# Chosen tokens: probabilities divided before their transposes, the attention result made transposed by four heads side by side, the down product in one piece

## The chip, the cores and the metric

The kernel runs on one core of one Trainium2 chip. A core has five engines with a queue each, which meet only through semaphores: TensorE (PE; its weight loads are shown apart as PEld), VectorE (DVE), ScalarE (ACT), GpSimd (POOL) and SyncE (SP), which here only starts DMAs. The metric is the device time of one execution in microseconds, the median of several runs.

## The reference, cut to what matters

The program has two halves. The first is a state-space scan over 16 batches of 1024 tokens by 512 features; the change does not touch it. The second takes, in each of the 16 batches, the 127 tokens with the highest router weight, and runs one transformer layer over them (b = 16, kc = 127, H = 16 heads of hd = 32, D = 512, F = 2048):

```python
x_sel = x[bidx, sel_idx]                      # 127 rows of each batch
hn = rmsnorm(x_sel, ln1)                      # x is layer-normed ahead of this
q = rope(heads(hn @ wq), pos_sel)
kk = rope(heads(hn @ wk), pos_sel)
v = heads(hn @ wv)
sc = jnp.einsum('bhqd,bhkd->bhqk', q, kk) / np.sqrt(hd) + m_sel[:, None]
a = jax.nn.softmax(sc, axis=-1)
o = jnp.einsum('bhqk,bhkd->bhqd', a, v).transpose(0, 2, 1, 3).reshape(b, kc, d) @ wo
x1 = x_sel + o
x2 = x1 + jax.nn.gelu(rmsnorm(x1, ln2) @ w1) @ w2
proc = x2 * w_sel[..., None]                  # scattered back to its rows
```

All is float32, and matrix products are float32 too.

## The kernel before, in words

`scan_phase` is the first half. `ffn_phase` is the second, and the change lies in it alone. It keeps all weights in SBUF and works on one batch a step. One `body(i, par)` for each engine is written out by hand, in the order in which that engine is to issue; a loop of `steps` runs it for i = 0 to 16. Step i does the attention of batch i and, interleaved with it, the MLP of batch i - 1: `attention(i)` is false in step 16 alone, `mlp(i)` in step 0 alone, and `final(i)` is true in step 15, which has no next batch to get ready. The middle steps run from a hardware loop, two at a time. `par` is the parity, and chooses between two buffers; `pm` is the other one.

There is no scheduler. Every PSUM bank has a list of its uses in a step (`BANK_USES`), and a pair of semaphores: `full[bank]` counts how often PE has filled it, `free[bank]` how often a reader has given it back. `fill` makes PE wait until the use before has been read, `filled` makes a reader wait until the use is there. `use_number` turns a step and a use into the count.

In a step PE does this, in this order (`turn` is four 128x128 transposes, `product` four accumulated matmuls):

- q and k of batch i, from `hnT`, which the step before left;
- `h2T` and the four up products `up0` to `up3` (MLP of batch i - 1); ACT makes the gelu of each;
- transposes of the gathered mask rows and of q and k, the mask product and the scores of all 16 heads (`scores`, four heads beside each other, each on 32 rows of the array);
- 16 transposes of the gelu's result (`gT0` to `gT3`), then three quarters of the down product: `down(i, 0)` to `down(i, 2)`;
- 16 transposes of the exponentials `prob` (`aT`), which wait for ACT's exp (`exp_ready`), and the four of the next batch's normed rows (`turn_hn`);
- the last quarter `down(i, 3)`, and meanwhile ACT and DVE copy one half each of the transposed exponentials to `probT`;
- `o`: 16 matmuls, head by head, with `probT` (127 x 128) held in the array and 32 columns of the values `vsb` moved through. The result has tokens on partitions and is not yet divided by the softmax sum;
- half of the next batch's `values`, the four transposes of `osb`, the other half of `values`, and the output product `attn` = `oT` times `w_o`.

DVE in the meantime adds the mask to the scores, takes the row maximum and subtracts it; ACT takes exp; DVE runs `prepare(i + 1)` (layer norm and RMS norm of the next batch's rows, in turn with ACT's `prepare`), copies its half of `probT`, sums `prob` over keys (`mx[:, 1]`), takes the reciprocal, and then divides while it copies `o` from PSUM to `osb`. ACT copies the transposed `osb` to `oT` (`copy(i, "oT", oT[:])`), after the next batch's values (`copy_v`). The semaphore `soft` counts four steps of the softmax in each batch (`SOFT = 4`); `o_ready` counts two: the `probT` copy of DVE and the division.

After `attn`, DVE adds the residual, DVE and ACT make the second norm (`h2`), and the step is at its end; q and k of the next step cover that on PE.

Of the kernel before, what the change touches and what calls it, by code (L numbers as in the profile page):

```python
# [7 lines left out]
ALU = mybir.AluOpType  # L8
# [7 lines left out]
P = 128  # L16
# [65 lines left out]
def scan_phase(nc, semaphores, x, A_log, w_xproj, w_dt, dt_b, D_col, router_w, router_b, ident_c, nsum_c, bc_dram,  # L82
# [824 lines left out]
KS = K - 1  # L907
# [13 lines left out]
    "t1": ["h2T", "up1", "up3", "GT1", "gT1", "gT3", "oT"],  # L921
# [23 lines left out]
def ffn_phase(nc, semaphores, w_dram, x1_dram, out, mask, pos, wq, wk, wv, wo, w1, w2, ln1, ln2, ident_c, sel16_c, token_c,  # L945
              batch_c, inv_c):

    with ExitStack() as ctx:
# [51 lines left out]
        osb = sb("osb", [P, D])  # L1000
# [174 lines left out]
        def _(pe):  # L1175
# [54 lines left out]
            def body(i, par):  # L1230
# [40 lines left out]
                if mlp(i):  # L1271
                    for j in range(4):

                        bank = BANK_OF[f"up{j}"]
                        pe.wait_ge(free[bank], use_number(i, f"up{j}") + 1)
                        fill(pe, i, f"gT{j}")
                        turn(BANK_OF[f"gT{j}"], act_up[:, j * HALF:(j + 1) * HALF])
                    fill(pe, i, "down")
                    for j in range(3):
                        down(i, j)  # L1280
                if attention(i):

                    pe.wait_ge(exp_ready, a + 1)
                    fill(pe, i, "aT")
                    for h in range(H):
                        last = pe.transpose(banks["s"][0:KS, h // 4, (h % 4) * P:(h % 4 + 1) * P], prob[:, h, 0:KS],  # L1286
                                            ident[:])
                    last.then_inc(full["s"], 1)
                    if not final(i):
                        turn_hn(i)  # L1290
                if mlp(i):

                    down(i, 3)
                if attention(i):

                    pe.wait_ge(free["s"], use_number(i, "aT") + 1)
                    pe.wait_ge(o_ready, a * 2 + 1)

                    pe.wait_ge(free["t0"], use_number(i - 1, "v") + 1)
                    fill(pe, i, "o")  # L1300
                    for h in range(H):
                        hd = 4 * (h % 4) + h // 4
                        last = pe.matmul(one["m0"][:, hd * HD:(hd + 1) * HD], probT[0:KS, h, :],  # L1303
                                         vsb[0:KS, par, hd * HD:(hd + 1) * HD], start=True, stop=True)
                    last.then_inc(full["m0"], 1)

                    if not final(i):
                        values(i, range(0, 2))
                    pe.wait_ge(o_ready, a * 2 + 2)
                    fill(pe, i, "oT")  # L1310
                    turn("t1", osb)
                    if not final(i):
                        values(i, range(2, KD))
                    pe.wait_ge(free["t1"], use_number(i, "oT") + 1)
                    fill(pe, i, "attn")
                    product("m1", oT, lambda k: w_o[:, k, :], KD)
# [5 lines left out]
        def _(act):  # L1322
# [52 lines left out]
            def body(i, par):  # L1375
# [14 lines left out]
                if attention(i):  # L1390
# [11 lines left out]
                    if not final(i):  # L1402
                        copy_ahead(i, pm)
                        copy_v(i, pm)
                    copy(i, "oT", oT[:])
# [10 lines left out]
        def _(dve):  # L1416
# [41 lines left out]
            def prepare(a, par):  # L1458

                v = v1[:, par, :]  # L1460
                at = a * NORM
                c = lambda j: v[:, j:j + 1]
# [16 lines left out]
                V.scalar_tensor_tensor(c(0), c(6), 0.25, c(5), ALU.mult, ALU.add).then_inc(norm, 1)  # L1479
                dve.wait_ge(norm_act, a * 5 + 2)  # L1480
                newton(norm, at + 8, c(2), c(0), c(3), c(4), c(6))
                V.tensor_scalar(xn[:, par, :], xg[:, par, :], c(1), c(6), ALU.subtract, ALU.mult).then_inc(norm, 1)

                dve.wait_ge(norm_act, a * 5 + 3)
                V.tensor_scalar(c(9), c(8), 1.0 / D, 1e-6, ALU.mult, ALU.add).then_inc(norm, 1)
# [15 lines left out]
            prepare(0, 0)  # L1501
# [60 lines left out]
            def body(i, par):  # L1562
                a, m, pm = i, i - 1, 1 - par
                if attention(i):
# [30 lines left out]
                    if not final(i):  # L1595
                        prepare(i + 1, pm)
                if attention(i):
                    at = a * SOFT
                    dve.wait_ge(full["s"], use_number(i, "aT") + 1)
                    V.tensor_copy(probT[0:KS, 8:16, :],  # L1600
                                  banks["s"][0:KS, 2:4, :].rearrange("p j (k t) -> p (j k) t", t=P))\
                     .then_inc(o_ready, 1)
                    dve.wait_ge(exp_ready, a + 1)
                    V.tensor_reduce(mx[:, 1, :], prob[:, :, 0:KS], AX.X, ALU.add).then_inc(soft, 1)
                    dve.wait_ge(soft, at + 3)
                    V.reciprocal(mx[:, 2, :], mx[:, 1, :]).then_inc(soft, 1)
                    bank = filled(dve, i, "o")
                    dve.wait_ge(soft, at + 4)

                    V.tensor_tensor(osb[:].rearrange("p (k j e) -> p k j e", k=4, j=4),  # L1610
                                    one[bank].rearrange("p (k j e) -> p k j e", k=4, j=4),
                                    mx[:, 2, :].rearrange("p (j k) -> p k j", j=4).unsqueeze(3)
                                    .to_broadcast([P, 4, 4, HD]), ALU.mult).then_inc(o_ready, 1)
                    dve.wait_ge(o_ready, a * 2 + 2)
                    dve.sem_inc(free[bank], 1)
# [31 lines left out]
SOFT = 4  # L1647
# [77 lines left out]
```

## Time and profile before

| | us |
|---|---|
| median of 3 runs | 4733.67 (4727.59 to 4733.85) |
| the profiled execution's own time | 4730.44 |
| its span on the core | 4728.3 |
| PE busy in the span | 2806.7 (59%) |
| DVE busy | 3868.9 (82%) |
| ACT busy | 2752.0 (58%) |
| POOL busy | 3543.6 (75%) |

The shares are means over both halves. The page's second part cuts the span into 40 slices of 118 us and gives each engine's busy share in tenths: up to about 3640 us DVE and POOL stand at 9 and PE at 4 to 6, and in the last eight slices PE stands at 9 and POOL at 0. The granted clock of PE, in tenths of full speed, is in the same part: 5 to 6 in the first half, 9 in the second. The second half of the program begins near 3640 us, its steps near 3736 us. The rows further down are from the second half, except where their heading says otherwise.

### The profile page before, as it was taken

What the parts mean: (1) busy time and instruction counts of PE and PEld (TensorE: products, weight loads), DVE (VectorE), ACT (ScalarE), POOL (GpSimd) and SP (SyncE); (2) the same over time, 40 slices, a digit from 0 to 9 for tenths busy, and PEclk for the clock granted to TensorE, in tenths of its full rate; (3) what the DMA queues carried; (4) which work ended last, traced back from release to release, by engine and by line L of the source; (5) the groups of instructions that cost most, each with busy time, mean ns of one, the idle gap of its engine ahead of it and who ended that gap; (6) DMA issues with size and microseconds to landing.
All of it is one profiled execution on the core that took longest, in us unless ns stands there. A gap on an engine that the chain in (4) does not pass through costs nothing. (4 is left out here: it accounts for less than half of the span.)

```text
span 4728.3 us, 57323 instructions
## 1 busy us (share of the span) xinstructions
PE 2806.7 (59%) x15590; PEld 1068.8 (23%) x15590; DVE 3868.9 (82%) x3306; ACT 2752.0 (58%) x4103; POOL 3543.6 (75%) x1796
## 2 busy tenths in 40 slices
PE   3555464546464645555454546464642399999997
PEld 1111111111121111111111111111110255555553
DVE  3999999999999999999999999999997644444442
ACT  5676766766767667676766766767754222222221
POOL 4999999999999999999999999999995100000000
PEclk7556565656565656556565656565655599999998
DMA  4454545364544545454545364545533200000000
GB/s 101 96 130 116 142 104 154 85 160 100 147 114 129 131 112 133 111 130 116 141 105 155 82 160 100 146 112 133 135 93 114 82 14 18 18 18 18 18 18 7
DMA packets 198209, 472.73 MB, mean 100 GB/s; under 512 B 60688, under 2 KB 61200, under 8 KB 197088
## 3 DMA queue, kind: packets, MB, share of 16 engines
q1 hardware_dynamic: 177136, 452.11, 37.8%
q0 software_dynamic: 20736, 16.88, 1.3%
q8 instruction: 120, 1.97, 0.2%
q14 instruction: 217, 1.78, 0.1%
HBM read 126.83 MB, written 73.43 MB: 42 GB/s over the span
## 5 line engine op out<-in xcount | busy, mean ns | idle before, releaser
L879 POOL TENSOR_TENSOR ch<-hid,cmat 128x1024 f32<-128x1024 f32 x1024 | 2387.2, 2354 | 101.0 <-DVE hid L733 84.1
L733 DVE TENSOR_TENSOR_SCAN hid<-decay,inp 128x1024 f32<-128x1024 f32 x1024 | 2289.2, 2274 | 96.3 <-ACT decay L600 94.2
L600 ACT ACTIVATE decay<-delr,a_neg 128x1024 f32<-128x1024 f32 x1024 | 1136.7, 1112 | 811.8 <-DVE hid L733 801.0
L399 PE MATMUL ps_y<-ch,nsum 128*32 128x256 f32 x8192 | 1000.3, 588 | 854.9 <-POOL ch L879 850.9
L722 DVE TENSOR_TENSOR inp<-dx,bmat 128x1024 f32<-128x1024 f32 x832 | 959.3, 1211 | 63.2 <-ACT dx L608 63.2
L399 PEld LDWEIGHTS ps_y<-ch,nsum 128*32 128x32 f32 x8192 | 249.0, 143 | 1591.5 <-POOL ch L879 1364.2
L408 PE MATMUL ps_y<-ident,ysb 128*128 128x128 f32 x512 | 168.9, 431 | 683.3 <-ACT ysb L615 666.7
L844 POOL TENSOR_TENSOR inp<-dxr,bmat 128x1024 f32<-128x1024 f32 x192 | 452.4, 2356 | 0.0
L1133 POOL DMA_INDIRECT out_rows<-row,idx_out x16 | 41.1, 2570 | 458.9 <-issue 252.4
L394 PE MATMUL ps_y<-xhT,dskip 128*32 128x256 f32 x2048 | 271.9, 623 | 142.5 <-DVE xr L743 142.5
L408 PEld LDWEIGHTS ps_y<-ident,ysb 128*128 128x128 f32 x512 | 71.3, 196 | 909.4 <-ACT ysb L615 865.9
L608 ACT ACTIVATE dx<-dxr 128x1024 f32<-128x1024 f32 x256 | 260.8, 1019 | 3.0 <-DMA dxr<-dxT 3.0
L382 PE MATMUL aux<-xpT,dtw 64*128 64x512 f32 x256 | 238.9, 1030 | 21.2 <-ACT dxT L510 20.5
L1195 PE MATMUL ps_t<-w,h2T 128*128 128x512 f32 x512 | 226.1, 600 | 11.9 <-ACT h2T L1334 11.9
L1219 PE MATMUL ps_m<-w,gT 128*128 128x512 f32 x512 | 224.9, 592 | 0.0
L1099 POOL COPY idx_x<-cols_i 128x1 uint32 (+1 forms) x16 | 4.7, 297 | 252.8 <-DMA out_rows<-row,idx_out 175.4
L547 ACT ACTIVATE squares<-xr,m 128x512 bf16<-128x512 f32 x256 | 181.7, 713 | 1.0
L853 POOL TENSOR_TENSOR tu<-tu,te 128x1024 f32<-128x1024 f32 x64 | 150.8, 2356 | 36.4 <-ACT tu L524 36.4
L1573 DVE TENSOR_SCALAR GT<-ps_t 128x512 f32<-128x512 f32 x32 | 22.0, 691 | 185.7 <-PE ps_t L1190 185.7
L743 DVE TENSOR_TENSOR xr<-xr,ps_y 128x256 f32<-128x256 f32 x256 | 106.3, 415 | 76.0 <-PE ps_y L408 68.3
L541 ACT ACTIVATE squares<-xr 128x512 bf16<-128x512 f32 x256 | 157.4, 617 | 14.3 <-DVE xr L743 14.2
L1099 POOL COPY idx_m<-cols_i 128x1 uint32 (+1 forms) x16 | 2.9, 180 | 207.3 <-PE ps_t L1190 204.7
(167 smaller groups left out, 3921.7 us busy)
## 6 DMA issues: line engine op xcount, KB each, us to landing
dxr<-dxT SPq DMA_DIRECT2D x1024, 128.0 KB, 2.4
delr<-delT SPq DMA_DIRECT2D x1024, 128.0 KB, 2.4
xr<-in_x SPq DMA_DIRECT2D x32, 1024.0 KB, 5.5
bmat<-b_and_c SPq DMA_DIRECT2D x256, 128.0 KB, 3.4
cmat<-b_and_c SPq DMA_DIRECT2D x256, 128.0 KB, 2.9
x_rows<-xr SPq DMA_DIRECT2D x16, 2048.0 KB, 7.6
out_rows<-xr SPq DMA_DIRECT2D x32, 1024.0 KB, 4.3
w<-in_w SPq DMA_DIRECT2D x2, 4096.0 KB, 23.7
```

The source lines that it names most:

```text
L382: pe.matmul(aux[:], dtw[:, k * P:(k + 1) * P], xpT[0:R, h * HALF:(h + 1) * HALF], start=True, stop=True).then_inc(aux_full, 1)
L394: pe.matmul(ps_y[q * CH:(q + 1) * CH, 0:2 * P], dskip[:, k, c % NT * CH:(c % NT + 1) * CH], xhT[:, i, j, q * 2 * P:(q + 1) * 2 * P], start ...
L399: last = pe.matmul(ps_y[q * CH:(q + 1) * CH, 0:2 * P], nsum[:], ch[:, g, q * 2 * P:(q + 1) * 2 * P], start=False, stop=(g == GROUPS - 1))
L408: last = pe.transpose(ps_y[:, (2 + t) * P:(3 + t) * P], ysb[:, t * P:(t + 1) * P], ident[:])
L600: nc.scalar.activation(decay[:, g % 2, :], delr[:, c % 2, :], ACT.Exp, scale=a_neg[:, i:i + 1])\
L608: nc.scalar.activation(dx[:], dxr[:, c % 2, :], ACT.Copy).then_inc(dx_ready, 1)
L722: nc.vector.tensor_tensor(inp[:, g, :], dx[:], bmat[:, g, :], ALU.mult).then_inc(inp_ready, 1)
L733: nc.vector.tensor_tensor_scan(hid[:, g, :], decay[:, g % 2, :], inp[:, g, :], 0.0, ALU.mult, ALU.add).then_inc(hid_ready, 1)
L844: nc.gpsimd.tensor_tensor(inp[:, OWN, :], dxr[:, c % 2, :], bmat[:, OWN, :], ALU.mult)\
L879: nc.gpsimd.tensor_tensor(ch[:, g, :], hid[:, g, :], cmat[:, g, :], ALU.mult).then_inc(ch_ready, 1)
L1195: last = pe.matmul(one[bank], xT[:, k, :], w(k), start=(k == 0), stop=(k == n - 1))
L1219: last = pe.matmul(one["m1"], gT[:, k, :], w_2[:, k, :], start=(k == 0), stop=(k == F // P - 1))
```

## The change

It has four parts.

1. The exponentials are divided by their sum before PE transposes them. DVE's sum and reciprocal move ahead, and a multiply of the whole `prob` by the reciprocals (128 x 2032 elements) is new; PE's transposes `aT` wait for it (`soft` at 5, where they waited for `exp_ready`). `prepare` on DVE is cut into four functions, whose instructions are laid around the sum and the multiply; ACT's part of it is as it was.
2. `o` changes its operands' roles: 32 columns of `vsb` are held in the array and the 128 columns of `probT` are moved. The result of head 4k + j lands on partitions 32j to 32j + 31, columns 128k to 128k + 127 of bank `m0`: it is made transposed. Four heads follow each other on four different quarters of the array's columns.
3. The four transposes of `osb`, the buffer, DVE's dividing copy and the use `oT` of bank `t1` are gone; ACT copies bank `m0` straight to `oT`, now before `copy_v`. `values` is issued in one piece.
4. `down(i, 3)` is issued with the other three quarters, ahead of `aT`.

```diff
--- before.py
+++ after.py
@@ -918,7 +918,7 @@
 AHEAD = ("hnT", "v")
 BANK_USES = {
     "t0": ["up0", "up2", "GT0", "gT0", "gT2", "hnT", "v"],
-    "t1": ["h2T", "up1", "up3", "GT1", "gT1", "gT3", "oT"],
+    "t1": ["h2T", "up1", "up3", "GT1", "gT1", "gT3"],
     "m0": ["q", "qT", "mask", "o"],
     "m1": ["k", "kT", "down", "attn"],
     "s": ["scores", "aT"],
@@ -997,7 +997,6 @@
         msel = sb("msel", [P, K])
         prob = sb("prob", [P, H, K])
         probT = sb("probT", [P, H, P])
-        osb = sb("osb", [P, D])
         oT = sb("oT", [P, KD, P])
         x1f = sb("x1f", [P, 2, D])
         h2 = sb("h2", [P, 2, D])
@@ -1276,11 +1275,11 @@
                         fill(pe, i, f"gT{j}")
                         turn(BANK_OF[f"gT{j}"], act_up[:, j * HALF:(j + 1) * HALF])
                     fill(pe, i, "down")
-                    for j in range(3):
+                    for j in range(4):
                         down(i, j)
                 if attention(i):
 
-                    pe.wait_ge(exp_ready, a + 1)
+                    pe.wait_ge(soft, a * SOFT + 5)
                     fill(pe, i, "aT")
                     for h in range(H):
                         last = pe.transpose(banks["s"][0:KS, h // 4, (h % 4) * P:(h % 4 + 1) * P], prob[:, h, 0:KS],
@@ -1288,30 +1287,23 @@
                     last.then_inc(full["s"], 1)
                     if not final(i):
                         turn_hn(i)
-                if mlp(i):
-
-                    down(i, 3)
                 if attention(i):
 
                     pe.wait_ge(free["s"], use_number(i, "aT") + 1)
-                    pe.wait_ge(o_ready, a * 2 + 1)
+                    pe.wait_ge(o_ready, a + 1)
 
                     pe.wait_ge(free["t0"], use_number(i - 1, "v") + 1)
                     fill(pe, i, "o")
-                    for h in range(H):
-                        hd = 4 * (h % 4) + h // 4
-                        last = pe.matmul(one["m0"][:, hd * HD:(hd + 1) * HD], probT[0:KS, h, :],
-                                         vsb[0:KS, par, hd * HD:(hd + 1) * HD], start=True, stop=True)
+                    for k in range(KD):
+                        for j in range(4):
+                            last = pe.matmul(one["m0"][j * HD:(j + 1) * HD, k * P:(k + 1) * P],
+                                             vsb[0:KS, par, (4 * k + j) * HD:(4 * k + j + 1) * HD],
+                                             probT[0:KS, 4 * j + k, :], start=True, stop=True)
                     last.then_inc(full["m0"], 1)
 
                     if not final(i):
-                        values(i, range(0, 2))
-                    pe.wait_ge(o_ready, a * 2 + 2)
-                    fill(pe, i, "oT")
-                    turn("t1", osb)
-                    if not final(i):
-                        values(i, range(2, KD))
-                    pe.wait_ge(free["t1"], use_number(i, "oT") + 1)
+                        values(i)
+                    pe.wait_ge(free["m0"], use_number(i, "o") + 1)
                     fill(pe, i, "attn")
                     product("m1", oT, lambda k: w_o[:, k, :], KD)
 
@@ -1401,8 +1393,9 @@
                                          ACT.Copy).then_inc(free["s"], 1)
                     if not final(i):
                         copy_ahead(i, pm)
+                    copy(i, "o", oT[:])
+                    if not final(i):
                         copy_v(i, pm)
-                    copy(i, "oT", oT[:])
                     v = v1[:, par, :]
                     act.wait_ge(norm2, a * NORM2 + 1)
                     nc.scalar.activation(sq2[:], x1f[:, par, :], ACT.Square, accum_out=v[:, 16:17])\
@@ -1455,11 +1448,13 @@
                 V.tensor_tensor(r, r0, t, ALU.mult).then_inc(sem_, 1)
                 dve.wait_ge(sem_, at + 4)
 
-            def prepare(a, par):
-
-                v = v1[:, par, :]
+            def column(par, j):
+                return v1[:, par, j:j + 1]
+
+            def statistics(a, par):
+
                 at = a * NORM
-                c = lambda j: v[:, j:j + 1]
+                c = lambda j: column(par, j)
                 dve.wait_ge(x_in[par], (a - par) * 8 + 16)
                 if not (isinstance(a, int) and a == 0):
 
@@ -1477,12 +1472,24 @@
                 V.tensor_scalar(c(5), c(5), 1.0 / D, EPS, ALU.mult, ALU.add).then_inc(norm, 1)
                 dve.wait_ge(norm, at + 7)
                 V.scalar_tensor_tensor(c(0), c(6), 0.25, c(5), ALU.mult, ALU.add).then_inc(norm, 1)
+
+            def centre(a, par):
+
+                at = a * NORM
+                c = lambda j: column(par, j)
                 dve.wait_ge(norm_act, a * 5 + 2)
                 newton(norm, at + 8, c(2), c(0), c(3), c(4), c(6))
                 V.tensor_scalar(xn[:, par, :], xg[:, par, :], c(1), c(6), ALU.subtract, ALU.mult).then_inc(norm, 1)
 
+            def mean_square(a, par):
+
                 dve.wait_ge(norm_act, a * 5 + 3)
-                V.tensor_scalar(c(9), c(8), 1.0 / D, 1e-6, ALU.mult, ALU.add).then_inc(norm, 1)
+                V.tensor_scalar(column(par, 9), column(par, 8), 1.0 / D, 1e-6, ALU.mult, ALU.add).then_inc(norm, 1)
+
+            def scale_rows(a, par):
+
+                at = a * NORM
+                c = lambda j: column(par, j)
                 dve.wait_ge(norm_act, a * 5 + 5)
                 dve.wait_ge(norm, at + 14)
                 newton(norm, at + 14, c(11), c(9), c(12), c(13), c(14))
@@ -1498,7 +1505,10 @@
 
 
             dve.wait_ge(cols_done, 5)
-            prepare(0, 0)
+            statistics(0, 0)
+            centre(0, 0)
+            mean_square(0, 0)
+            scale_rows(0, 0)
             make_base(0, 0)
             dve.wait_ge(idxbc_full, 1)
             V.tensor_copy(idx_bc[:].rearrange("p b k -> p (b k)"),
@@ -1593,26 +1603,24 @@
                     V.tensor_tensor(p3, p3, mx[:, 0, :].unsqueeze(2).to_broadcast([P, H, KS]), ALU.subtract)\
                      .then_inc(soft, 1)
                     if not final(i):
-                        prepare(i + 1, pm)
-                if attention(i):
-                    at = a * SOFT
+                        statistics(i + 1, pm)
+                        centre(i + 1, pm)
+                    dve.wait_ge(exp_ready, a + 1)
+                    V.tensor_reduce(mx[:, 1, :], p3, AX.X, ALU.add).then_inc(soft, 1)
+                    dve.wait_ge(soft, at + 3)
+                    V.reciprocal(mx[:, 2, :], mx[:, 1, :]).then_inc(soft, 1)
+                    if not final(i):
+                        mean_square(i + 1, pm)
+                    dve.wait_ge(soft, at + 4)
+
+                    V.tensor_tensor(p3, p3, mx[:, 2, :].unsqueeze(2).to_broadcast([P, H, KS]), ALU.mult)\
+                     .then_inc(soft, 1)
+                    if not final(i):
+                        scale_rows(i + 1, pm)
                     dve.wait_ge(full["s"], use_number(i, "aT") + 1)
                     V.tensor_copy(probT[0:KS, 8:16, :],
                                   banks["s"][0:KS, 2:4, :].rearrange("p j (k t) -> p (j k) t", t=P))\
                      .then_inc(o_ready, 1)
-                    dve.wait_ge(exp_ready, a + 1)
-                    V.tensor_reduce(mx[:, 1, :], prob[:, :, 0:KS], AX.X, ALU.add).then_inc(soft, 1)
-                    dve.wait_ge(soft, at + 3)
-                    V.reciprocal(mx[:, 2, :], mx[:, 1, :]).then_inc(soft, 1)
-                    bank = filled(dve, i, "o")
-                    dve.wait_ge(soft, at + 4)
-
-                    V.tensor_tensor(osb[:].rearrange("p (k j e) -> p k j e", k=4, j=4),
-                                    one[bank].rearrange("p (k j e) -> p k j e", k=4, j=4),
-                                    mx[:, 2, :].rearrange("p (j k) -> p k j", j=4).unsqueeze(3)
-                                    .to_broadcast([P, 4, 4, HD]), ALU.mult).then_inc(o_ready, 1)
-                    dve.wait_ge(o_ready, a * 2 + 2)
-                    dve.sem_inc(free[bank], 1)
                 if mlp(i):
 
                     bank = filled(dve, i, "down")
@@ -1644,7 +1652,7 @@
 NORM = 19
 NORM2 = 7
 ROPE = 12
-SOFT = 4
+SOFT = 5
 TOPK = 3 * (K // 8) + 5
 ANGLE = 9
 FOLDED = 3 * KD + KD
```

PE in step 1, from the transposes of the gelu's result (`act_up`) to the output product; `w` here is `w_2`. Before:

```order
L1190 MATMUL ps_t<-identf,act_up 128x128 x16
L1219 MATMUL ps_m<-w,gT 128x512 x12
L1286 MATMUL ps_s<-identf,prob 127x128 x16
L1190 MATMUL ps_t<-identf,hn 128x128 x4
L1219 MATMUL ps_m<-w,gT 128x512 x4
L1303 MATMUL ps_m<-vsb,probT 128x32 x16
L1211 MATMUL ps_t<-w_qkv,hnT 128x512 x2
L1190 MATMUL ps_t<-identf,osb 128x128 x4
L1211 MATMUL ps_t<-w_qkv,hnT 128x512 x2
L1195 MATMUL ps_m<-w_o,oT 128x512 x4
```

The same place of PE after the change:

```order
L1189 MATMUL ps_t<-identf,act_up 128x128 x16
L1218 MATMUL ps_m<-w,gT 128x512 x16
L1285 MATMUL ps_s<-identf,prob 127x128 x16
L1189 MATMUL ps_t<-identf,hn 128x128 x4
L1299 MATMUL ps_m<-probT,vsb 32x128 x16
L1210 MATMUL ps_t<-w_qkv,hnT 128x512 x4
L1194 MATMUL ps_m<-w_o,oT 128x512 x4
```

The last four down matmuls have moved ahead of the transposes of `prob`, so nothing but the transposes of `hn` stands between those and the `o` matmuls; the four transposes of `osb` are gone, and the values are in one piece.

DVE in step 1, from the normed rows `xn` of the next batch to the residual of the MLP. Before:

```order
L1482 TENSOR_SCALAR xn<-xg,v 128x512
L1485 TENSOR_SCALAR v<-v 128x1
L1449 TENSOR_TENSOR v<-v 128x1
L1451 TENSOR_TENSOR v<-v 128x1
L1453 TENSOR_SCALAR v<-v 128x1
L1455 TENSOR_TENSOR v<-v 128x1
L1489 TENSOR_SCALAR hn<-xn,v 128x512
L1600 COPY probT<-ps_s 127x1024
L1604 TENSOR_REDUCE mx<-prob 128x16
L1606 RECIPROCAL mx<-mx 128x16
L1610 TENSOR_TENSOR osb<-ps_m,mx 128x512
L1619 TENSOR_TENSOR x1f<-ps_m,x1f 128x512
```

After:

```order
L1482 TENSOR_SCALAR xn<-xg,v 128x512
L1609 TENSOR_REDUCE mx<-prob 128x16
L1611 RECIPROCAL mx<-mx 128x16
L1487 TENSOR_SCALAR v<-v 128x1
L1616 TENSOR_TENSOR prob<-prob,mx 128x16x127
L1442 TENSOR_TENSOR v<-v 128x1
L1444 TENSOR_TENSOR v<-v 128x1
L1446 TENSOR_SCALAR v<-v 128x1
L1448 TENSOR_TENSOR v<-v 128x1
L1496 TENSOR_SCALAR hn<-xn,v 128x512
L1621 COPY probT<-ps_s 127x1024
L1627 TENSOR_TENSOR x1f<-ps_m,x1f 128x512
```

Sum, reciprocal and the new multiply now stand between `xn` and the end of the RMS norm, ahead of the `probT` copy; the dividing copy to `osb` is gone.

## Rows read from the trace of the kernel before

**Rows 1.** The page, part 2: tenths in 40 slices of 118 us

```profile
PE   3555464546464645555454546464642399999997
...
PEclk7556565656565656556565656565655599999998
```

**Rows 2.** In order of time, PE: start us, us, engine, line, operation [idle before]

```profile
4260.54 0.69 DVE L1632 TENSOR_TENSOR x1f<-ps_m,xn 128x512 f32<-128x512 f32 x1 [6.96 <-PE ps_m L1195]
...
4287.02 1.17 PE L1268 MATMUL ps_s<-qkT 32*128 32x127 f32 x32
...
4288.12 1.09 PE L1190 MATMUL ps_t<-identf,act_up 128*128 128x128 f32 x8
...
4290.51 10.47 PE L1219 MATMUL ps_m<-w,gT 128*128 128x512 f32 x24
...
4300.81 1.94 PE L1286 MATMUL ps_s<-identf,prob 128*127 128x128 f32 x16
...
4302.58 0.60 PE L1190 MATMUL ps_t<-identf,hn 128*128 128x128 f32 x4
...
4303.02 3.60 PE L1219 MATMUL ps_m<-w,gT 128*128 128x512 f32 x8
...
4306.45 3.66 PE L1303 MATMUL ps_m<-vsb,probT 127*128 127x32 f32 x32
4309.95 1.96 PE L1211 MATMUL ps_t<-w_qkv,hnT 128*128 128x512 f32 x4
...
4311.75 0.60 PE L1190 MATMUL ps_t<-identf,osb 128*128 128x128 f32 x4
...
4312.18 1.88 PE L1211 MATMUL ps_t<-w_qkv,hnT 128*128 128x512 f32 x4
...
4315.24 3.70 PE L1195 MATMUL ps_m<-w_o,oT 128*128 128x512 f32 x8 [1.18 <-ACT oT L1334]
...
4318.98 0.69 DVE L1632 TENSOR_TENSOR x1f<-ps_m,xn 128x512 f32<-128x512 f32 x1 [5.44 <-PE ps_m L1195]
```

**Rows 3.** The same view and step, DVE and ACT

```profile
4292.87 2.28 DVE L1593 TENSOR_TENSOR prob<-prob,mx 128x2032 f32<-128x2032 f32 x1
...
4295.18 1.90 ACT L1395 ACTIVATE prob<-prob 128x2032 f32<-128x2032 f32 x1 [2.58 <-DVE prob L1593]
...
4298.21 0.55 DVE L1482 TENSOR_SCALAR xn<-xg,v 128x512 f32<-128x512 f32 x1
...
4302.78 1.23 DVE L1600 COPY probT<-ps_s 127x1024 f32<-127x1024 f32 x1 [1.24 <-PE ps_s L1286]
...
4303.92 2.26 DVE L1604 TENSOR_REDUCE mx<-prob 128x16 f32<-128x2032 f32 x1
4306.22 0.25 DVE L1606 RECIPROCAL mx<-mx 128x16 f32<-128x16 f32 x1
```

**Rows 4.** The same view, PE in the scan

```profile
232.81 1.07 PE L399 MATMUL ps_y<-ch,nsum 128*32 128x256 f32 x16
233.81 1.10 PE L373 MATMUL aux<-xhT,xproj 128*96 128x512 f32 x2
```

**Rows 5.** Busy by stretch: PE, PEld, DVE, ACT, POOL, granted clock, DMA share, GB/s

```profile
4246.33:4250.30 3.97, 3.97 (x34) 3.77 (x33) 0.29 (x2) 0.00 (x0) 0.00 (x0) 1.00 0.00 0
4250.50:4253.80 3.30, 3.30 (x8) 1.65 (x8) 2.41 (x4) 0.00 (x0) 0.00 (x0) 0.50 0.00 0
```

**Rows 6.** In order of time, step 0

```profile
3768.11 3.78 PE L1286 MATMUL ps_s<-identf,prob 128*127 128x128 f32 x16 [8.95 <-ACT prob L1395]
...
3789.61 0.69 DVE L1632 TENSOR_TENSOR x1f<-ps_m,xn 128x512 f32<-128x512 f32 x1 [9.40 <-PE ps_m L1195]
```

**Rows 7.** In order of time, step 15, from its start to its end

```profile
4612.91 0.69 DVE L1632 TENSOR_TENSOR x1f<-ps_m,xn 128x512 f32<-128x512 f32 x1 [5.78 <-PE ps_m L1195]
...
4664.16 6.73 PE L1195 MATMUL ps_m<-w_o,oT 128*128 128x512 f32 x8 [0.69 <-ACT oT L1334]
...
4670.93 0.69 DVE L1632 TENSOR_TENSOR x1f<-ps_m,xn 128x512 f32<-128x512 f32 x1 [6.54 <-PE ps_m L1195]
```

## The prediction, made before the changed kernel had been run

> **What bounds the kernel now.** I read the busy tenths of the 40 slices first. The change lies in the second half of the program, the last eight slices, where PE stands at 9 tenths and the granted clock at 9 [rows 1]: there PE is the engine to shorten, and what another engine gains is worth nothing unless PE waits for it. Next I read one middle step in order of time. Its end is DVE's residual add behind the output product; two of them are 4260.54 and 4318.98, so a step takes 58.44 us [rows 2]. There are 16 such adds; from the one of step 0 (3789.61) to that of step 14 (4612.91) are 14 steps and 823.3 us [rows 6, 7], 5.1 more than 14 x 58.44. That rest is in the third view, the busy time by stretch: behind the 32-column matmuls of `o` the granted clock was once 0.50 for the whole of 4250.50 to 4253.80, PE busy throughout [rows 5]. This is its 1.2 GHz level instead of 2.4, for a little over 3.3 us, and about 1.7 us are lost. Three such falls make up the 5.1.
>
> Within the step [rows 2], PE spends 10.30 us on 24 down matmuls (0.429 each), 1.77 on the transposes of `prob`, 0.44 on those of `hn`, 3.43 on the last 8 down matmuls, 3.50 on `o`, 1.80 on half the values, 0.43 on the transposes of `osb`, then 3.06 until `attn` starts, of which 1.72 are four matmuls of values and 1.34 is waiting for ACT's `oT` (the row says 1.18; the rest lies in how ends are modelled).
>
> **The change part by part.** I lay out the same step anew, from the down product's start at 4290.51, with durations of [rows 2, 3].
>
> *Down in one piece.* 32 x 0.429 = 13.73: it ends at 4304.24. Nothing of it is saved or added. What it takes away is the cover of the `probT` copies, below.
>
> *Sum, reciprocal, multiply ahead of the transposes.* Exp ends at 4297.08. DVE's `xn` ends at 4298.76, so the sum starts then: 2.26 to 4301.02. Reciprocal 0.25, one small column operation 0.15, and the handing over between dependent ones: 4301.5. The multiply does not stand in the trace; its nearest row is the subtraction L1593, a tensor by a broadcast column over the same 128 x 2032 elements, 2.28 us. It ends at 4303.8. PE starts a transposed block's first weight load about 0.43 before the matmul, here at 4303.81, so the multiply arrives just as it is wanted. I cost this at 0 to 0.1 a step. The cover is the down product alone; were each of the two long DVE passes 10% slower, the wait would be 0.4 us. A lower bound below nothing is excluded, since PE cannot start the transposes before the down product is through. The rest of the RMS norm (four small operations, `hn`) is then done near 4305.2, before PE wants it at 4306.01.
>
> *The `probT` copies lose their cover.* The transposes of `prob` end at 4306.01, those of `hn` at 4306.45. DVE's copy began 0.20 behind the end of the transposes before (4302.78 against 4302.58) and took 1.23; so it now ends at 4307.44, and PE's `o` starts at about 4307.50. PE waits 1.05 us where it waited for nothing. In DVE's queue behind the copy stands the MLP's residual add, which has nobody waiting who is not already behind `o`.
>
> *`o` four heads side by side.* 32 matmul instructions as before. Before, each took 0.109 (3.50 / 32), though only 32 columns moved: the load of 128 columns of weights sets it. Now 128 columns move and 32 are loaded. The nearest row is the scores: 32 instructions of 127 columns, four heads on different rows, from 4287.02 to the next start at 4288.12, 1.10 us [rows 2]. That four quarters of the columns run side by side too is in the scan: 16 matmuls of 256 columns, 128 rows high and 32 columns wide, take 1.00 us from start to next start at full clock [rows 4], where one behind the other they would take 16 x 0.215 = 3.4. Four groups there, eight groups of half the length here: 8 x 0.11 plus about 0.15 to 0.2 of filling and draining = 1.1. The ends are 1.0 and, if nothing overlapped, 3.5. I take 1.10, so -2.40.
>
> The Trainium skill says (TensorEngine Tiling (Array Packing), "Key Properties") that changing the tiling mode drains TensorE. The scores' row bears this out: 8 x 0.11 = 0.88 against 1.10 measured, and the same 0.2 is already in the 1.10 that I use.
>
> *`osb` and its transposes gone.* 4 x 0.108 = 0.43 on PE, -0.43. The wait for `oT`, -1.34: ACT's copy of `m0` starts 0.2 behind `o` and takes 0.59, and all 8 value matmuls (3.43) now lie over it; `copy_v` stands behind it and no longer delays it. With the wait goes the slow start of `attn`: 3.74 from its start to the add, where 8 x 0.429 and a lag of 0.2 make 3.63. What is next is PE's own work.
>
> *Sum for a middle step.* `o` from 4307.50 to 4308.60, values to 4312.03, `attn` to 4315.46, the add at 4315.66 instead of 4318.98: -3.3. By terms: -2.40 - 0.43 - 1.34 - 0.1 - 0.1 + 1.05 = -3.3. ACT's and DVE's work after `attn` is as it was, under q and k of the next step. For 14 steps -46.
>
> *The falls of the clock.* They came behind `o`, when PE had issued narrow matmuls for 3.5 us [rows 5]. That stretch shrinks to 1.1 with all quarters in use. Its successor is a shorter one of transposes, 1.05 us of waiting and `o`. The 1.34 us of waiting for `oT` had no fall behind it in this step. So I take all three falls as gone, -5; the ends are 0 and -5.
>
> The Trainium skill says (TensorE: Matmul & The Clock Gate, "Part 4: PE-mode transpose") that transposes do not count as busy for the clock gate. This speaks against the change, which puts 2.2 us of transposes beside the new wait. The trace does not bear it out so far: the transposes from 4300.81 to 4303.02 ran and were followed by matmuls at 0.429. By that rule the falls would stay or come more often.
>
> *Step 0* has no down product, so the DVE chain is bare: exp ended at 3768.1, and `xn` follows it by 1.13 + 0.55 [rows 3], then sum, reciprocal, multiply, about 5.1. The transposes start at 3774.8 instead of 3768.11 [rows 6], 6.7 late. Behind them PE needs 11.3 at full clock (1.77 + 0.44 + 1.05 + 1.1 + 3.43 + 3.43) and up to 21 at half; it took 21.5 before, mostly at half (16 transposes 3.78 against 1.94). So the end moves by something between -3 and +6; with half of it at full clock, +2.5.
>
> *Step 15* has no next batch. The transposes start 1 us after where the down product let them, the wait is 1.5 instead of 1.05, and ACT's copy of `oT` is bare, 0.85. Counted as above, `attn` starts 2.3 us earlier. It ran at half clock (6.73 against the 3.70 of [rows 2]) [rows 7]; I leave that as it was: -2.3; at full clock it would be -5.3. Step 16 and all before step 0 are unchanged.
>
> **The sum.** 4730.44 - 46 - 5 + 2.5 - 2.3 = 4679.6 for the profiled execution's own time (its span of 4728.3 and the 2.1 around it, which nothing here touches). That execution lies 3.2 below the median of the runs, so 4683 is predicted.
>
> **The rivals.**
>
> *The falls stay,* on the new stretch of transposes, wait and `o`, once in four steps: the sum without its -5, 4688. For it: step 0, with waits of this size, was largely at half clock. Against it: no fall but behind the 32-column stretch. If the 3.3 us of transposes and waiting brought a fall in every step, it would be 15 x 1.7 = 25 on top of the 4683, 4708; the 2.2 us of transposes of [rows 2] had none behind them. This second case is what the Trainium skill's rule on transposes, above, would lead to.
>
> *The heads do not run side by side* (the values must be loaded afresh for every head, on all 128 rows): `o` stays at 3.5, 14 x 2.4 = 34 lost, 4717. Against it: the loads of `ch,nsum` are fresh ones too and overlap [rows 4].
>
> *The multiply comes late.* If sum and multiply become the path because a pass runs slower than its row, now that ACT's square runs beside it, PE waits behind the down product. From 3.3 us late it eats the whole gain of a middle step. At twice their rows' durations, 4.5 late, steps would cost 1.2 more than before: 4733.7 + 15 x 1.2 + 7 in step 0 - 5 of the falls = 4754, slower than before. For it: the slack is practically nothing. Against: the three rows of this size (2.26 to 2.28) do not differ. A small lateness of 0.5 is far more likely and gives 4690.
>
> **How the numbers follow.** Forecast 0.74, its own range 4677 to 4688; falls stay 0.11; falls in every step 0.04; no overlap of heads 0.04; multiply 0.5 late or so 0.05; slower than before 0.02. The range 4672 to 4702 has step 0 and `attn` of step 15 at full clock below, and above the falls staying together with a half-clock step 0 or a late multiply; the two large rivals stay outside. A difference of 0.2% (9.5 us) is what a measurement can tell: faster 0.97, same 0.01, slower 0.02.
>
> **What would show it.** `o` should read about 1.1 us from start to next start for 32 instructions; one wait of 1.0 to 1.1 before it, released by DVE's `probT` copy; no wait before `attn`; the transposes of `prob` starting 13.7 to 13.9 behind the down product's start; two adds 55.2 us apart; no clock of 0.50 between steps 1 and 14. Step 0's transposes should start near 3774.8. The prediction is wrong if the multiply is the releaser of a long PE wait, if `o` takes over 2 us, or if the clock falls as often as before.

## The result, and the profile after

The changed kernel takes 4677.7 us (median of 5 runs, 4673.9 to 4682.1) against 4733.7 before. The ratio is 0.9883 with a 95% interval of 0.9871 to 0.9894, a gain of 50 to 61 us. Predicted were 4683, between 4672 and 4702. The profiled execution has a span of 4675.8 us, 52.5 less than before.

A middle step of PE in order of time (the columns are those of [rows 2]), and the adds at its two ends:

```profile
4233.29 0.69 DVE L1640 TENSOR_TENSOR x1f<-ps_m,xn 128x512 f32<-128x512 f32 x1 [5.98 <-PE ps_m L1194]
...
4263.26 13.90 PE L1218 MATMUL ps_m<-w,gT 128*128 128x512 f32 x32
...
4276.99 1.94 PE L1285 MATMUL ps_s<-identf,prob 128*127 128x128 f32 x16
4278.77 0.60 PE L1189 MATMUL ps_t<-identf,hn 128*128 128x128 f32 x4
...
4280.52 1.08 PE L1299 MATMUL ps_m<-probT,vsb 127*32 127x128 f32 x32 [1.15 <-ACT hnT L1326]
...
4281.53 3.70 PE L1210 MATMUL ps_t<-w_qkv,hnT 128*128 128x512 f32 x8
...
4285.07 3.60 PE L1194 MATMUL ps_m<-w_o,oT 128*128 128x512 f32 x8
...
4288.70 0.69 DVE L1640 TENSOR_TENSOR x1f<-ps_m,xn 128x512 f32<-128x512 f32 x1 [6.14 <-PE ps_m L1194]
```

The step is 55.41 us where [rows 2] has 58.44. `o` starts at 4280.52 and the values behind it at 4281.53, so its 32 instructions take 1.01; they took 3.50. `attn` has no wait ahead of it any more. In the trace's single records the instructions of `o` start in eight groups of four, about 7 ns apart in a group (4280.519, .526, .532, .539) and 0.109 from group to group (the next starts at 4280.647). One wait is new, ahead of `o`. The row names ACT's `hnT`; by time it is DVE's copy, in the next rows. Here are DVE's sum, multiply, `hn` and `probT` copy of the same step:

```profile
4270.96 0.55 DVE L1482 TENSOR_SCALAR xn<-xg,v 128x512 f32<-128x512 f32 x1
4271.42 2.26 DVE L1609 TENSOR_REDUCE mx<-prob 128x16 f32<-128x2032 f32 x1
...
4274.00 2.28 DVE L1616 TENSOR_TENSOR prob<-prob,mx 128x2032 f32<-128x2032 f32 x1
...
4276.96 0.49 DVE L1496 TENSOR_SCALAR hn<-xn,v 128x512 f32<-128x512 f32 x1
...
4278.97 1.22 DVE L1621 COPY probT<-ps_s 127x1024 f32<-127x1024 f32 x1 [1.52 <-PE ps_s L1285]
```

The multiply ends at 4276.28, 0.7 before PE's transposes at 4276.99, which start where the down product lets them. The copy ends at 4280.19, and `o` is 0.33 behind that. PE's queue shows what lies between: the wait for the copy ends at 4280.23, then come two register additions, at 4280.336 and 4280.428, for the two waits that stand next in the code, and the first weight load at 4280.512. The unrolled steps have no such additions.

Busy time from step 0's end of the low clock to the end of step 15 (columns as in [rows 5]): the granted clock is 1.00, where [rows 5] shows one of the three falls. A single fall would still leave such a rounded mean at 1.00; what rules it out is that the 14 steps are all 55.17 or 55.41 long.

```profile
3783.00:4620.00 837.00, 794.17 (x3492) 420.13 (x3484) 409.62 (x762) 239.92 (x418) 75.38 (x84) 1.00 0.07 18
```

Steps 0 and 15 in order of time, against [rows 6, 7]:

```profile
3776.81 3.78 PE L1285 MATMUL ps_s<-identf,prob 128*127 128x128 f32 x16 [15.39 <-DVE prob L1616]
...
3790.25 0.69 DVE L1640 TENSOR_TENSOR x1f<-ps_m,xn 128x512 f32<-128x512 f32 x1 [7.74 <-PE ps_m L1194]
...
4565.51 0.69 DVE L1640 TENSOR_TENSOR x1f<-ps_m,xn 128x512 f32<-128x512 f32 x1 [6.11 <-PE ps_m L1194]
...
4614.29 3.70 PE L1194 MATMUL ps_m<-w_o,oT 128*128 128x512 f32 x8 [0.71 <-ACT oT L1326]
...
4618.03 0.69 DVE L1640 TENSOR_TENSOR x1f<-ps_m,xn 128x512 f32<-128x512 f32 x1 [4.24 <-PE ps_m L1194]
```

Where the 52.5 us went, by the distances between these adds: steps 1 to 14 fell from 823.3 to 775.3, that is 48.0 (43.0 of it the steps themselves and 5.1 the three falls); step 15 from 58.0 to 52.5, that is 5.5; step 0, from its exp to its add, from 23.5 to 21.8, that is 1.6. Against that, the profiled execution came to step 0's exp 2.3 us later, of which 1.4 lie in the scan, which the change does not touch, and it ran 0.4 longer behind step 15.

### The profile page after: what moved, and what is told of

The parts are those of the page before. It is cut to its first block and busy times, and to the rows that moved or that the text cites. A ratio compares the mean times of both kernels' runs of the same rounds, so it can differ in the third digit from the quotient of the medians.

```text
span 4675.8 us, 57243 instructions
## 1 busy us (share of the span) xinstructions
PE 2747.1 (59%) x15526; PEld 1014.5 (22%) x15526; DVE 3888.9 (83%) x3306; ACT 2753.9 (59%) x4103; POOL 3546.3 (76%) x1796
## 3 DMA queue, kind: packets, MB, share of 16 engines
q8 instruction: 119, 1.95, 0.2%
```

## The experiments

The first four kernels ran on one chip, the other three on another, each beside runs of the kernel before. The theory going in was the prediction's sum; the rivals stand in each expectation.

**One part alone: down in one piece.** From the kernel before:

```diff
-                    for j in range(3):
+                    for j in range(4):
                         down(i, j)
...
-                if mlp(i):
-
-                    down(i, 3)
```

> The kernel before with one part of the change alone: the last quarter of the down product moved ahead of the transposes of prob. Theory (the quarter was the cover of the probT copies): PE waits 1.1 us more ahead of o in the unrolled steps and up to 1.3 in the loop's steps, so a middle step takes 59.5 to 59.7 instead of 58.44 and the time rises by 15 to 18 us, to about 4750. Rival (the cover is worth nothing, because exp or DVE's sum would have bounded it anyway, or the wait for oT shrinks by as much): a step of 58.4 and no change. On the clock: the narrow o product is as before, so falls to 0.50 behind it are expected still.

Measured: 4780.3 us, ratio 1.0119 (1.0089 to 1.0149): slower by 48, and not by 18 (one of the four runs took 4807.2, the others 4778.5 to 4781.3; the ratio takes it in). A step in order of time:

```profile
4221.34 0.69 DVE L1629 TENSOR_TENSOR x1f<-ps_m,xn 128x512 f32<-128x512 f32 x1 [6.93 <-PE ps_m L1195]
...
4265.04 1.94 PE L1286 MATMUL ps_s<-identf,prob 128*127 128x128 f32 x16
4266.81 0.60 PE L1190 MATMUL ps_t<-identf,hn 128*128 128x128 f32 x4
4268.56 4.04 PE L1300 MATMUL ps_m<-vsb,probT 127*128 127x32 f32 x32 [1.15 <-ACT hnT L1331]
4272.41 3.39 PE L1211 MATMUL ps_t<-w_qkv,hnT 128*128 128x512 f32 x4
...
4282.87 0.69 DVE L1629 TENSOR_TENSOR x1f<-ps_m,xn 128x512 f32<-128x512 f32 x1 [6.68 <-PE ps_m L1195]
```

and the busy time around the end of `o` in it:

```profile
4268.50:4271.80 3.30, 3.24 (x29) 3.24 (x30) 2.16 (x2) 0.02 (x1) 0.00 (x0) 1.00 0.00 0
4272.00:4275.20 3.20, 3.20 (x7) 1.65 (x8) 2.04 (x3) 0.00 (x0) 0.00 (x0) 0.50 0.00 0
```

The wait ahead of `o` is the expected one: 4268.56 less the 4267.25 at which the transposes of `hn` end (0.44 behind their start) is 1.3. But the step is 61.53, and the missing 1.7 to 1.8 come with a fall of the clock to 0.50 right behind `o`, now in every step from 1 to 14, and not in three of the 14; in the last few of them it lasted longer. So the cover of the copies was real, and the fall was the dearer half of losing it.

**Down cut as before, in the changed kernel.**

```diff
-                    for j in range(4):
+                    for j in range(3):
                         down(i, j)
...
+                if mlp(i):
+
+                    down(i, 3)
                 if attention(i):
```

> The changed kernel with its down product cut again as before, the last quarter behind the transposes of hn. Theory (the multiply ahead of the transposes needs the whole down product as its cover): the multiply is done 42.99 us into a step, three quarters of down at 40.27, so PE waits 2.7 to 2.8 before the transposes, wins back the 1.3 to 1.55 before o, and a loop step takes 56.9 instead of 55.41; the time rises by about 20 us to 4698. Rival (the lost cover of the copies is the larger price): a step of 54.1, the time 4659.

Measured: 4719.1 us, ratio 0.9972 (0.9960 to 0.9983). That is 41 above the changed kernel, where 20 were expected. A step with a fall in it, in order of time, and its busy time by stretch:

```profile
4197.88 0.69 DVE L1643 TENSOR_TENSOR x1f<-ps_m,xn 128x512 f32<-128x512 f32 x1 [5.61 <-PE ps_m L1194]
...
4241.10 3.67 PE L1285 MATMUL ps_s<-identf,prob 128*127 128x128 f32 x16 [2.79 <-DVE prob L1619]
4244.61 0.60 PE L1189 MATMUL ps_t<-identf,hn 128*128 128x128 f32 x4
4245.05 3.60 PE L1218 MATMUL ps_m<-w,gT 128*128 128x512 f32 x8
4248.57 1.08 PE L1302 MATMUL ps_m<-probT,vsb 127*32 127x128 f32 x32
...
4256.76 0.69 DVE L1643 TENSOR_TENSOR x1f<-ps_m,xn 128x512 f32<-128x512 f32 x1 [5.44 <-PE ps_m L1194]
```

```profile
4237.50:4241.00 3.50, 0.81 (x2) 0.00 (x0) 3.44 (x5) 0.41 (x2) 0.00 (x0) 1.00 0.00 0
4241.20:4244.40 3.20, 3.20 (x15) 3.20 (x16) 0.83 (x4) 0.00 (x0) 0.00 (x0) 0.50 0.00 0
```

Steps without a fall take 57.13, near the 56.9 expected: PE waits 2.8 for the multiply and nothing ahead of `o`. Steps with one take 58.7 to 60.2, and ten of the steps from 1 to 14 have one, here behind the 2.8 us of waiting. So parts 1 and 4 belong together: divided ahead, the transposes need nearly the whole down product before them (the fifth experiment shows how nearly).

**The heads in turn.** The loops of `o` exchanged, so that heads on the same quarter of the columns follow each other:

```diff
-                    for k in range(KD):
-                        for j in range(4):
+                    for j in range(4):
+                        for k in range(KD):
```

> The changed kernel with the two loops of the o product exchanged: the four heads on one quarter of the columns follow each other, so neighbours do not differ in their quarter. Same 32 instructions and the same result. Theory (what made o short is four heads side by side): about 0.107 to 0.11 an instruction, o takes 3.4 to 3.5 us instead of 1.0, a loop step 57.8 to 57.9, and the time rises by some 36 us to 4714. Rival (it is the smaller weight load, 32 columns instead of 128, that made it short): o stays at 1.0 to 1.5, a rise of under 8 us. On the clock: if the falls came because only 32 columns were moved at a time, none is expected here; if because a quarter of the array was in use, they come back, about 1.7 us each.

Measured: 4699.8 us, ratio 0.9929 (0.9913 to 0.9946), 22 above the changed kernel, between both expectations. `o` and what follows it:

```profile
4293.77 2.46 PE L1299 MATMUL ps_m<-probT,vsb 127*32 127x128 f32 x32 [1.15 <-ACT hnT L1326]
4296.15 3.70 PE L1210 MATMUL ps_t<-w_qkv,hnT 128*128 128x512 f32 x8
```

`o` takes 2.38 us, and not 3.5 or 1.0. The starts of single instructions show why: those on one quarter follow each other at 0.109, as far apart as in the kernel before, so the narrower weight load alone gains nothing there. But where the loop passes to the next quarter, an instruction starts 6 ns after the one before (3839.600 and 3839.606), and for some while two rows of starts run interleaved. So the order of the heads is worth 1.37 us a step; of the 2.49 saved in `o`, 1.1 come even in the poor order, from this partial overlap, and the rest with the good one. The clock did not fall once in steps 1 to 14, although each quarter stood idle for most of `o`.

**Two waits ahead.** `o` had four waits in PE's queue; the two that are long satisfied move up:

```diff
                     fill(pe, i, "aT")
+                    pe.wait_ge(free["t0"], use_number(i - 1, "v") + 1)
+                    fill(pe, i, "o")
...
-                    pe.wait_ge(free["t0"], use_number(i - 1, "v") + 1)
-                    fill(pe, i, "o")
```

> The changed kernel with two of the four waits that PE runs ahead of o (for the values' bank and for o's own bank, both long satisfied) moved ahead of the transposes of prob. Theory (in the hardware loop each wait value is computed by PE's queue in turn, and this arithmetic now stands in the open between the probT copies and o): the loop's steps fall from 55.41 by 0.15 to 0.25, towards the 55.17 of the unrolled ones, 2 to 3 us in all. Rival (the 0.24 us between loop steps and unrolled ones comes from the copies or from instruction fetch): steps stay at 55.41.

Measured: 4676.8 us, ratio 0.9881 (0.9865 to 0.9898). The two adds and `o`:

```profile
4233.24 0.69 DVE L1639 TENSOR_TENSOR x1f<-ps_m,xn 128x512 f32<-128x512 f32 x1 [5.79 <-PE ps_m L1194]
...
4280.28 1.08 PE L1298 MATMUL ps_m<-probT,vsb 127*32 127x128 f32 x32 [0.97 <-DVE probT L1620]
...
4288.47 0.69 DVE L1639 TENSOR_TENSOR x1f<-ps_m,xn 128x512 f32<-128x512 f32 x1 [5.96 <-PE ps_m L1194]
```

The loop's steps take 55.23 instead of 55.41. That is 2.2 us over 12 steps; the total cannot tell it from no change, the steps can. The wait is now released by the `probT` copy in name too. In PE's queue the two additions are gone from behind it: the wait ends at 4280.178 and the first weight load starts at 4280.253, 0.075 later, where it was 0.28 (4280.230 to 4280.512). Loop steps and unrolled ones (55.22) are now alike, as the theory wants; the unrolled ones, though, were 55.17 before the edit.

**What is left: the wait for the copies.** On top of the two waits, DVE's sum goes ahead of the centring (`centre`), and the last two instructions of the down product go behind the transposes of `prob` (`down` gets two more arguments, the first block and the one past the last). A third, small edit puts `mean_square` behind the multiply:

```diff
                     for j in range(3):
                         down(i, j)
+                    down(i, 3, 0, 3)
...
+                if mlp(i):
+                    down(i, 3, 3, 4)
...
                         statistics(i + 1, pm)
-                        centre(i + 1, pm)
                     dve.wait_ge(exp_ready, a + 1)
                     V.tensor_reduce(mx[:, 1, :], p3, AX.X, ALU.add).then_inc(soft, 1)
+                    if not final(i):
+                        centre(i + 1, pm)
...
-                    if not final(i):
-                        mean_square(i + 1, pm)
...
                     if not final(i):
+                        mean_square(i + 1, pm)
                         scale_rows(i + 1, pm)
```

> The version with the two waits moved ahead, and two more edits: DVE's sum goes ahead of the centring of the next batch's rows (it waited 1.5 us for its turn), and the last two matmul instructions of the down product come behind the transposes of prob. Theory (what is left to win is the wait for the probT copies, as long as the multiply is done when 30 of the 32 down instructions are): the multiply ends at 42.8 in the step instead of 42.99, transposes from 42.85, o starts at 46.2 instead of 47.04, a middle step takes 54.35 to 54.5 instead of 55.22, and the time falls by 11 to 13 us to about 4665. Rival (the multiply comes later in this order, or hn does): o starts no sooner than 46.9 and the time stays within 3 us of 4677.

Measured: 4665.0 us, ratio 0.9856 (0.9840 to 0.9872). A step in order of time:

```profile
4227.63 0.69 DVE L1643 TENSOR_TENSOR x1f<-ps_m,xn 128x512 f32<-128x512 f32 x1 [5.79 <-PE ps_m L1194]
...
4257.59 13.04 PE L1218 MATMUL ps_m<-w,gT 128*128 128x512 f32 x30
...
4267.88 2.27 DVE L1618 TENSOR_TENSOR prob<-prob,mx 128x2032 f32<-128x2032 f32 x1
4270.47 2.03 PE L1288 MATMUL ps_s<-identf,prob 128*127 128x128 f32 x16
...
4272.34 1.02 PE L1218 MATMUL ps_m<-w,gT 128*128 128x512 f32 x2
...
4273.20 0.60 PE L1189 MATMUL ps_t<-identf,hn 128*128 128x128 f32 x4
4273.91 1.08 PE L1302 MATMUL ps_m<-probT,vsb 127*32 127x128 f32 x32
```

The transposes start 42.84 us into the step, where 30 down instructions of 0.429 end, the multiply having ended 0.3 before them; `o` starts at 46.28 and a step of the loop takes 54.47 to 54.62. The wait ahead of `o` is not gone but short: the transposes of `hn` end at 4273.64 and `o` starts at 4273.91, 0.27 later, where the changed kernel has 1.32. This version beats both kernels: 66 us faster than the one before, and about 13 faster than the changed one, 12 of which lie beyond the two waits. No run separates the edits from each other.

**Without the division.** The second experiment's kernel with the multiply left out and the transposes waiting for exp, so the softmax stays undivided:

```diff
-                    pe.wait_ge(soft, a * SOFT + 5)
+                    pe.wait_ge(exp_ready, a + 1)
...
-                    dve.wait_ge(soft, at + 4)
-
-                    V.tensor_tensor(p3, p3, mx[:, 2, :].unsqueeze(2).to_broadcast([P, H, KS]), ALU.mult)\
-                     .then_inc(soft, 1)
...
-SOFT = 5
+SOFT = 4
```

> The changed kernel with the down product cut as before and without the multiply by the reciprocals: the softmax is left undivided (that part of the computation is missing), and PE's transposes wait for exp alone. It measures what the division ahead of the transposes costs. Theory (the parts on o save 4.3 us a step, and the division ahead takes 1.3 of it by way of the lost cover, nothing else): transposes start at 40.3 again, no wait before o, a middle step takes 54.1 against 55.41 and against 57 to 59 with the multiply in this order; no falls of the clock; the time is about 4659. Rival (the rest of the difference between 58.44 and 55.41 lies elsewhere, DVE's other work for one): a step of 55 or more.

Measured: 4666.5 us, ratio 0.9861 (0.9845 to 0.9878), a step of 54.82 to 54.92 and no fall. The part on `o` is borne out, but the step is 0.7 above expectation: with the sum now ahead of it, `hn` came late and PE waited about 0.6 for it (the transposes of `prob` end at 4265.01). The rows show it:

```profile
4265.58 0.66 PE L1189 MATMUL ps_t<-identf,hn 128*128 128x128 f32 x4 [0.41 <-DVE hn L1499]
4266.08 3.60 PE L1218 MATMUL ps_m<-w,gT 128*128 128x512 f32 x8
```

As it stands, this kernel's step is 0.5 to 0.6 shorter than the changed kernel's and 0.3 longer than the fifth experiment's (54.5). That is not the price of dividing ahead, since this kernel pays for its late `hn`. Without that wait its step would be about 54.2, an estimate from the rows above; against this, dividing ahead costs the changed kernel about 1.2 us a step, near the 1.3 of the theory, and the fifth experiment's kernel about 0.3.

**More columns moved in `o`, for the clock.** The first experiment's kernel, but each `o` instruction moves 128 columns of the values, so the attention result is another:

```diff
-                        last = pe.matmul(one["m0"][:, hd * HD:(hd + 1) * HD], probT[0:KS, h, :],
-                                         vsb[0:KS, par, hd * HD:(hd + 1) * HD], start=True, stop=True)
+                        c = min(hd * HD, D - P)
+                        last = pe.matmul(one["m0"][:, c:c + P], probT[0:KS, h, :],
+                                         vsb[0:KS, par, c:c + P], start=True, stop=True)
```

> The kernel before with down whole (a step of 61.54, a fall of the clock in every step), and with each of the o product's 32 instructions moving 128 columns of the values instead of 32; the extra columns overwrite neighbours, so the output of the attention is another. An instruction keeps its length, 0.11 us, since the weight load sets it. Theory (the falls follow from few moved columns over the 3.5 us of o): no or few falls, a step of 59.8, the time 4752 to 4757. Rival (they follow from the wait and the length of the stretch): a fall in every step, 61.5, the time 4780.

Measured: 4742.2 us, ratio 1.0022 (1.0013 to 1.0032). In order of time, and the busy time over steps 1 to 15:

```profile
4310.18 0.60 PE L1190 MATMUL ps_t<-identf,hn 128*128 128x128 f32 x4
4311.93 3.83 PE L1301 MATMUL ps_m<-vsb,probT 127*128 127x128 f32 x32 [1.15 <-ACT hnT L1332]
4315.60 1.88 PE L1211 MATMUL ps_t<-w_qkv,hnT 128*128 128x512 f32 x4
```

```profile
3787.00:4680.00 893.00, 834.90 (x3526) 462.45 (x3524) 389.16 (x759) 236.09 (x412) 72.69 (x84) 1.00 0.06 16
```

`o` takes 3.67 where it took 3.50, with the wait's 1.3 ahead of it, and the clock does not fall once: steps 2 to 13 are all 59.84 or 59.85 long. A step is 59.85: that is 58.44 + 1.3 and 0.1, the first experiment without its falls. Four times the columns moved in the same time, and the kernel is 38 us faster by the medians than the first experiment's. The two ran on different chips, on which the kernel before took 4732.6 and 4730.8, and their runs do not overlap (4737.4 to 4745.6 here, 4778.5 to 4807.2 there).

## Why the prediction was right

The forecast case came true, by its own mechanism and close to its size: 4679.6 was the sum for the profiled execution, 4677.7 its time. Step by step:

- **`o` side by side**, -2.40: measured -2.49 (3.50 to 1.01): eight groups at 0.109 make 0.87, and 0.14 are left for filling and draining, where 0.15 to 0.2 were put. Shown to be the order of the heads for 1.37 of it, by the heads in turn. Its rival, no overlap, is out.
- **`osb`, its transposes and the wait for `oT`**, -0.43 and -1.34: both gone, values and `attn` follow each other without a wait.
- **The lost cover**, +1.05: the step of the sum that was mis-sized. Unrolled steps, at 55.17, bear it out; the loop's 12 steps pay 0.24 more. The prediction counted the copy and a handing over of 0.06, and left out that in the loop the values to wait for are worked out in PE's queue: what stood under matmuls before now stands in the open. The two additions are in the trace of PE's queue, and moving their waits ahead took 0.18 back.
- **The multiply under the down product**, 0 to 0.1: measured 0. It had some 0.3 in hand at the point where PE begins to load, since DVE handed over between its operations faster than the prediction allowed. The second experiment shows what the prediction said of slack: without the last quarter, PE waits 2.8.
- **The middle step**: 55.41 for 55.14 forecast; 43.0 us over 14 steps for 46.
- **The falls**, -5: measured -5.1. The reason given, 32-column matmuls over a long stretch, was an inference then. Two kernels that differ in the columns moved by `o` now bear it out in that place: with 32 a fall in every step, with 128 none. The Trainium skill says (TensorE: Matmul & The Clock Gate, "Part 4: PE-mode transpose") that transpose mode does not count as busy in the same way and does not bring the full clock. The traces do not agree: the changed kernel puts 2.2 us of transposes and 1.3 of waiting in a row, and no fall came; and in the second experiment PE ran nothing but transposes from 4241.10 on, at the low level, and the clock was at 1.00 again in 4244.60 to 4245.00. But the second experiment, with 2.8 of waiting ahead of the transposes, had ten falls, so the rival of falls that stay was nearer than its 0.15 suggests.
- **Step 0**, +2.5: measured -1.6, the one sign that was wrong. The transposes start 8.4 us after the start of exp, where it was 1.95; 6.45 late for 6.7 forecast. But from before 3783 on PE had its full clock and kept it (the stretch shown above), so from there to the add it took 13.4 us, not the half-way 16; before it was 21.5.
- **Step 15**, -2.3: measured -5.5. The bound named for a full clock, -5.3, is what came: `attn` took 3.70 for 6.73. The kernel with the wide `o` has no low clock ahead of that add either, and the first experiment's has one, so the narrow `o` is the likely reason once more.

That the sum came within 2 us is partly luck, since its errors cancel: the gain was put 3.0 too high in the middle steps and 7.3 too low in steps 0 and 15, and the execution lost 2.7 outside the steps, which the change does not explain.

Not settled: why the falls in the first experiment got longer from the eleventh step on, and how a wait and narrow matmuls add up. Three of 14 steps had a fall without the wait and all 14 with it; no run separated the two.

## What to carry to other kernels

Read a busy PE twice: how long an instruction holds it and how many columns it moves in that time. Here a product with a small moved side cost its weight loads and, in some steps or in all, the clock; with the roles exchanged and neighbours on different quarters of the columns it took 1.01 us for 3.50. And what is placed under a copy can be sized: two of 32 down instructions behind the transposes, not eight and not none, hid all but 0.27 us of it and left the multiply its time.

## What the runs showed that was not expected

- With PE busy in 3.24 of 3.30 us, the granted clock still fell to its 1.2 GHz level right behind, in all 14 middle steps of one kernel. With 128 instead of 32 columns in each of the same 32 instructions it stayed at 2.4 GHz over 893 us.
- Matmuls of one quarter of the columns are 0.109 us apart, but a row of them overlaps in part with the next quarter's row: 2.38 us for 32, not 3.5.
- The loop's steps were 0.24 us longer than the unrolled ones once nothing covered the four waits ahead of `o`. Two register additions for the last two of them stand in PE's queue there; with these two waits moved ahead the loop's steps gained 0.18, the unrolled ones lost 0.05, and the difference is 0.01.
